# Eight experts' results: plain scatters into eight zeroed areas and additions on DVE, in place of accumulating scatters into one

## The reference

```python
k = max(MIN_CAPACITY, ceil(N * CAPACITY_FACTOR / E))   # N = 4096 tokens, E = 8: k = 1024
scores = softmax(xt @ Wr)
G, idx = top_k(scores.T, k)            # each expert takes its 1024 best tokens
X_in = xt[idx]
h = gelu(einsum('ekd,edh->ekh', X_in, W1) + b1)
X_e = einsum('ekh,ehd->ekd', h, W2) + b2
contrib = G[..., None] * X_e
out = zeros((N, D)).at[idx.reshape(-1)].add(contrib)
x = layernorm(x + out)
```

## Time and profile before

| | before |
|---|---|
| median of three runs | 719.66 us |
| span of the profiled execution | 715.9 us |
| PE busy | 577.3 us (81%) |
| DVE busy | 392.2 us (55%) |
| ACT busy | 324.2 us (45%) |
| POOL busy | 311.9 us (44%) |
| moved by DMA | 27.52 MB |

### The profile page before, as it was taken

One profiled execution on the slowest core, in us unless ns is written; L12 is line 12 of the kernel. 1 busy time (PEld: TensorE's weight loads), 2 busy tenths in 40 slices (PEclk: granted clock), 3 DMA queues, 4 the chain that ended last, 5 costly groups with the idle time before them and its releaser, 6 DMA issues.

```text
span 715.9 us, 11711 instructions
## 1 busy us (share of the span) xinstructions
PE 577.3 (81%) x3943; PEld 485.4 (68%) x3944; DVE 392.2 (55%) x942; ACT 324.2 (45%) x740; POOL 311.9 (44%) x309
## 2 busy tenths in 40 slices
PE   8899999999999999999998874017997688684700
PEld 7878889988998899889987761013775455552500
DVE  3237766675777677757766647886542240010206
ACT  3566755765676557656764321004431232131105
POOL 7103233322332333223323230017888788788756
PEclk9999999999999999999999995556997897897855
DMA  7000100001001000010000009001233233323347
GB/s 158 17 9 0 32 24 10 23 22 31 1 21 31 22 8 23 22 31 0 22 16 15 16 1 257 0 5 48 45 40 43 44 41 40 49 42 38 32 69 193
DMA packets 50066, 27.52 MB, mean 38 GB/s; under 512 B 14258, under 2 KB 46963, under 8 KB 50036
## 3 DMA queue, kind: packets, MB, share of 16 engines
q1 hardware_dynamic: 38144, 18.44, 9.8%
q0 software_dynamic: 11264, 8.66, 9.1%
q10 hardware_dynamic: 628, 0.03, 0.1%
HBM read 16.49 MB, written 10.62 MB: 38 GB/s over the span
## 4 chain that ended last, share of the span: by engine, by line
PE 42%; DVE 21%; POOL 15%; issue 13%; ACT 5%; DMA 3%; POOLq 0%; DVEq 0%; ACTq 0%
PE PS L1174 9%; POOL total L603 6%; POOL shared L593 6%; PE PS L1200 6%; PE PS L1414 6%; PE PS L1182 6%; PE PS L1396 3%; DVE csum L850 3%; PE PS L1191 3%; DVE pc L844 2%; DVE above L973 2%; DMA shared<-table,idx 2%; PE PS L1110 2%; DVE cmax L839 2%; ACT pc L672 1%
## 5 line engine op out<-in xcount | busy, mean ns | idle before, releaser
L568 POOL TENSOR_TENSOR pn<-pc,crcp 128x1232 f32<-128x1232 f32 x32 | 72.0, 2250 | 181.8 <-DVE crcp L853 181.8
L603 POOL DMA_INDIRECT total<-pn,idx x64 | 103.6, 1619 | 21.8 <-issue 18.0
L593 POOL DMA_INDIRECT shared<-table,idx x64 | 66.9, 1046 | 70.6 <-DVE idx L1031 51.4
L1174 PE MATMUL PS<-cT_hi,heads_hi 128*128 128x308 f32 x256 | 83.7, 327 | 1.2 <-DVE VOT L900 0.6
L652 ACT ACTIVATE shared<-PS 128x308 f32<-128x308 f32 (+1 forms) x144 | 62.0, 473 | 41.7 <-PE PS L1209 29.5
L1174 PE MATMUL PS<-cT_hi,heads_lo 128*128 128x308 f32 x256 | 77.9, 304 | 0.0
L1174 PE MATMUL PS<-cT_lo,heads_hi 128*128 128x308 f32 x256 | 77.4, 302 | 0.0
L1182 PE MATMUL PS<-shared,x1T 128*128 128x512 f32 (+1 forms) x192 | 72.4, 513 | 1.9 <-DVE pc L844 1.4
L1414 PEld LDWEIGHTS PS<-w,shared 128*128 128x128 f32 x512 | 71.0, 224 | 4.1 <-issue 3.8
L1414 PE MATMUL PS<-w,shared 128*128 128x128 f32 x512 | 72.2, 308 | 0.1
L787 ACT ACTIVATE shared<-PS,b1T 128x512 f32<-128x512 f32 x64 | 44.0, 687 | 60.3 <-PE PS L1396 60.3
(11 more groups left out here) (181 smaller groups left out, 1192.0 us busy)
## 6 DMA issues: line engine op xcount, KB each, us to landing
xin<-in_x SPq DMA_DIRECT2D x16, 128.0 KB, 2.1
table<-x SPq DMA_DIRECT2D x16, 128.0 KB, 2.0
total<-x SPq DMA_DIRECT2D x16, 128.0 KB, 1.9
w<-in_L_ffn_W SPq DMA_DIRECT2D x1, 2048.0 KB, 8.6
fin<-total SPq DMA_DIRECT2D x8, 256.0 KB, 5.0
out_x<-fin SPq DMA_DIRECT2D x8, 256.0 KB, 2.3
cin<-in_ctx SPq DMA_DIRECT2D x16, 77.0 KB
shared<-table,idx POOLq DMA_INDIRECT x64, 2.5
```

Source lines behind the costliest of these rows:

```text
L568: pool.tensor_tensor(pn[:, e, 0:HK].rearrange("p (h k) -> p h k", h=HEADS), pc[:, e, :].rearrange("p (h k) -> p h k", h=HEADS), crcp[:, e, ...
L593: pool.indirect_dma_start(xg[:, e % 3, h, :], None, table, bass.IndirectOffsetOnAxis(ap=idx[:, e, h:h + 1], axis=0)).then_inc(gathered[e % ...
L603: pool.indirect_dma_start(total, bass.IndirectOffsetOnAxis(ap=idx[:, e, h:h + 1], axis=0), ye[:, e % 2, h, :], None, compute_op=ALU.add).t ...
L1174: i = pe.matmul(bank[:, 0:4 * KEYS], w[a][:, h, :], cT[b][:, :], start=(n == 0), stop=(n == 2))
```

## The change

Each expert gets a DRAM area of its own, `spread[e]` (4096 rows of 128), in place of the one `total`. Eight parts:

1. POOL writes a tile `zeros` (128 x 512) among its constants, and ACT, behind its set-up copies and before its attention steps, issues eight DMAs that fill the eight areas with zeros from it, 2 MB each, in pieces of 2 KB (`cleared`).
2. SP no longer stores x2 to `total`, so `stored` counts 16 per pair, not 32.
3. Behind the gates' store SP loads x2 from `table` into `fin` in one DMA (`fin_x`).
4. The scatters are plain writes into `spread[e]`. Scatter(e) does not wait for scatter(e - 1) any more; scatter(0) waits for `cleared`. Two semaphores, by the parity of e, count the landings.
5. When the 8 blocks of expert e have landed, SP loads `spread[e]` in eight parts into `landed`, a view of `VOT` behind `yb`; from the second expert on each part waits until the same part of the expert before has been added.
6. DVE adds each part to `fin` (`add_landed`, 128 x 512): those of expert e - 2 stand in the program in halves behind `results(e, 0)` and `results(e, 1)`; those of expert 5 stand all before `last_results`, those of expert 6 behind it.
7. Those of expert 7 are put into the last loop, one part ahead of the statistics.
8. The eight loads of `total` at the end go.

```diff
+            act.wait_ge(consts, 19)
+            for e in range(E):
+                act.dma_start(spread[e].rearrange("(p a r) d -> p a (r d)", p=P, r=4),
+                              zeros[:, :].unsqueeze(1).to_broadcast([P, B // 4, 4 * P])).then_inc(cleared, 16)
             attention_steps(act, step)
...
                 sp.dma_start(tab[q, :, :, 0:P], x2[parity][:, :, :]).then_inc(stored[parity], 16)
-                sp.dma_start(sm[q], x2[parity][:, :, :]).then_inc(stored[parity], 16)
...
-            sp.wait_ge(scattered, 16 * SB * E)
-            rows = total.rearrange("(b t) d -> t b d", t=P)
-            for c in range(B // 4):
-                sp.dma_start(fin[:, 4 * c:4 * c + 4, :], rows[:, 4 * c:4 * c + 4, :]).then_inc(fin_in[c], 16)
+            sp.dma_start(fin[:, :, :], by_token[:, :, 0:P]).then_inc(fin_x, 16)
+
+            for e in range(E):
+                sp.wait_ge(scattered[e % 2], 16 * SB * (e // 2 + 1))
+                rows = spread[e].rearrange("(b t) d -> t b d", t=P)
+                for c in range(B // 4):
+                    if e:
+                        sp.wait_ge(landed_added, B // 4 * (e - 1) + c + 1)
+                    sp.dma_start(landed[:, 4 * c:4 * c + 4, :], rows[:, 4 * c:4 * c + 4, :]).then_inc(landed_in[c], 16)
...
-                if e:
-                    pool.wait_ge(scattered, 16 * SB * e)
+                if e == 0:
+                    pool.wait_ge(cleared, 16 * E)
                 for h in range(SB):
                     pool.wait_ge(ye_done, blocks_through(e, h))
-                    pool.indirect_dma_start(total, bass.IndirectOffsetOnAxis(ap=idx[:, e, h:h + 1], axis=0),
-                                            ye[:, e % 2, h, :], None, compute_op=ALU.add).then_inc(scattered, 16)
+                    pool.indirect_dma_start(spread[e], bass.IndirectOffsetOnAxis(ap=idx[:, e, h:h + 1], axis=0),
+                                            ye[:, e % 2, h, :], None).then_inc(scattered[e % 2], 16)
...
+            def add_landed(e, first, last):
+
+                if e == 0 and first == 0:
+                    dve.wait_ge(fin_x, 16)
+                for c in range(first, last):
+                    dve.wait_ge(landed_in[c], 16 * (e + 1))
+                    if e:
+                        dve.wait_ge(landed_added, B // 4 * (e - 1) + c + 1)
+                    dve.tensor_tensor(fin[:, 4 * c:4 * c + 4, :], fin[:, 4 * c:4 * c + 4, :],
+                                      landed[:, 4 * c:4 * c + 4, :], ALU.add).then_inc(landed_added, 1)
...
                 results(e, 0)
                 if e + 3 < E:
                     make_idx(e + 3)
+                if e >= 2:
+                    add_landed(e - 2, 0, B // 8)
                 results(e, 1)
+                if e >= 2:
+                    add_landed(e - 2, B // 8, B // 4)
+            add_landed(E - 3, 0, B // 4)
             last_results()
+            add_landed(E - 2, 0, B // 4)
...
+            add_landed(E - 1, 0, 1)
             for c in range(B // 4):
-                dve.wait_ge(fin_in[c], 16)
+                if c + 1 < B // 4:
+                    add_landed(E - 1, c + 1, c + 2)
+                dve.wait_ge(landed_added, B // 4 * (E - 1) + c + 1)
```

More of the change, by code:

```diff
@@ L297, in decoder_layer @@
         idx = sb("idx", [P, E, SB], I32)
-        yb = VOT[:, 0, 0:SB * P].rearrange("p (s d) -> p s d", s=SB)
+        votflat = VOT[:, :, :].rearrange("p b n -> p (b n)")
+        yb = votflat[:, 0:SB * P].rearrange("p (s d) -> p s d", s=SB)
+        landed = votflat[:, SB * P:SB * P + TOKENS].rearrange("p (b d) -> p b d", b=B)
+        zeros = sb("zeros", [P, 4 * P])
         stf = sb("stf", [P, B, 6])
@@ L373, in decoder_layer @@
         ye_done = sem("ye_done")
-        scattered = sem("scattered")
-        fin_in = [sem(f"fin_in{c}") for c in range(B // 4)]
+        cleared = sem("cleared")
+        scattered = [sem(f"scattered{k}") for k in range(2)]
+        fin_x = sem("fin_x")
+        landed_in = [sem(f"landed_in{c}") for c in range(B // 4)]
+        landed_added = sem("landed_added")
         fin_var = sem("fin_var")
@@ L383, in decoder_layer @@
         table = nc.dram_tensor("table", [TOKENS, ROW], F32, kind="Internal").ap()
-        total = nc.dram_tensor("total", [TOKENS, P], F32, kind="Internal").ap()
+        spread = [nc.dram_tensor(f"spread{e}", [TOKENS, P], F32, kind="Internal").ap() for e in range(E)]
         x_pairs = x.rearrange("(q e) t d -> q t e d", e=2)
@@ L487, in _ @@
             for k in range(2):
-                sp.wait_ge(stored[k], 32 * PAIRS // 2)
+                sp.wait_ge(stored[k], 16 * PAIRS // 2)
             sp.wait_ge(gates_done, 1)
-            sp.dma_start(table.rearrange("(b t) d -> t b d", t=P)[:, :, P:ROW], gates[:, :, :]).then_inc(gates_stored, 16)
-            sp.wait_ge(scattered, 16 * SB * E)
-            rows = total.rearrange("(b t) d -> t b d", t=P)
-            for c in range(B // 4):
-                sp.dma_start(fin[:, 4 * c:4 * c + 4, :], rows[:, 4 * c:4 * c + 4, :]).then_inc(fin_in[c], 16)
+            by_token = table.rearrange("(b t) d -> t b d", t=P)
+            sp.dma_start(by_token[:, :, P:ROW], gates[:, :, :]).then_inc(gates_stored, 16)
+            sp.dma_start(fin[:, :, :], by_token[:, :, 0:P]).then_inc(fin_x, 16)
[6 more added lines that the diff above has]
+                    sp.dma_start(landed[:, 4 * c:4 * c + 4, :], rows[:, 4 * c:4 * c + 4, :]).then_inc(landed_in[c], 16)
             for c in range(B // 4):
@@ L541, in _ @@
             pool.memset(keep[:, :, :], 1.0).then_inc(consts, 1)
+            pool.memset(zeros[:, :], 0.0).then_inc(consts, 1)
             pool.memset(onesb[:, :], 1.0).then_inc(consts, 1)
-            pool.wait_ge(consts, 18)
+            pool.wait_ge(consts, 19)
             pool.memset(keep[:, :, 0:1], 0.0).then_inc(consts, 1)
@@ L588, in gather @@
                     for k in range(2):
-                        pool.wait_ge(stored[k], 32 * PAIRS // 2)
+                        pool.wait_ge(stored[k], 16 * PAIRS // 2)
                 if e >= 3:
@@ L831, in second_norm @@
                     wait(dve, rstd2, 2 * q + e + 1)
-                    wait(dve, stored[par], 32 * earlier)
+                    wait(dve, stored[par], 16 * earlier)
                     dve.tensor_scalar(x2[par][:, e, :], r2[:, e, :], mv2[:, e, 0:1], rs2[:, e:e + 1],
@@ L1036, in last_results @@
                 e = E - 1
-                dve.wait_ge(scattered, 16 * SB * (e - 1))
+                dve.wait_ge(scattered[e % 2], 16 * SB * (e // 2))
                 for n in range(SB):
```

7 lines of the change are left out of this document (2 added, 5 removed).

## The result

The changed kernel takes 724.78 us, the median of four runs (723.59 to 726.51), beside 719.42 for the kernel before (718.54 to 719.85): a ratio of 1.0079, 95% interval 1.0055 to 1.0103. Slower, by 5.4 us where I had forecast 14.3. The profiled execution spans 722.5 us against 715.9. (Lines are renumbered: the gather is L604, the scatter L614, the additions L1083, the zeroing L775.)

The account below looks back on a forecast made before the run. Attention was taken as bound by PE, the expert stage by POOL's gathers and scatters, the tail by DVE. 715.9 - 23.5 + 38 = 730.4 us of span, plus 3.8, gave 734; range 697 to 746.

Parts of the forecast that it names:

- rival A: Before attention: ACT's queue fills and its zeroing issues hold it; 734 us, between 722 and 746; chance 0.62.
- the wait in front of the last scatter: Last expert: POOL waits 5 us, instead of 2.65, for expert 5's loads and additions before its final scatter.
- Scatter 0.945 us: Expert stage: a plain scatter takes POOL as long as a gather, 0.945 us instead of 1.552.
- Rival C: Expert stage: a plain scatter costs 1.55 us like the accumulating one, slower still, 769 or 733 us; chance 0.03.
- Stage 168.4 us: POOL, first gather to end of scatter 6: 168 us instead of 194.4, net -26 with 8 us of contention.
- Rival D: Expert stage: loads and additions bind, period stays 25 us, the 26 us gain is gone; 725 or 760; chance 0.03.
- The zeroing, +38: ACT before attention: eight 2 MB fills hold it until about 59 instead of 23.1, +36, plus 2 for PE.
- The rule: DMA issue on ACT: an issue ends when the backlog ahead has shrunk to 389 to 1611 packets.
- The restart of PE, +2: Start of attention: PE restarts from an idle spell with slower first matmuls, +2 us.
- Rival B: Before attention: the queue takes all eight fills at 0.5 us each, faster; 699 us, from 690 to 710; chance 0.28.
- The last expert, +2.5 (from -26 to -23.5): Final scatter and tail: longer wait and additions in the tail reduce the gain to -23.5 us, end at 692.4.
- Around the span: Whole kernel: the median of the runs lies 3.8 us above the profiled span.

Follow-up runs that it names:

- plain_in_before: Kernel before with the accumulation taken out of its scatters, areas, waits and stores unchanged; 715.8 us, ratio 0.9933 to the kernel before.
- small_adds: Changed kernel with each of DVE's 64 additions cut from 128x512 to 128x4; 752.5 us, ratio 1.0433 to the kernel before.
- after_again: Changed kernel run again unaltered on another chip; 758.0 us, ratio 1.048 to the kernel before.
- first comparison: First measurement of the changed kernel beside the kernel before, chip not on record; 724.8 us, ratio 1.0079.
- groups 1 to 5: Follow-up kernels, each group run on one chip beside the kernel before (2 and 3 shared a chip); the unaltered changed kernel took 751.8 to 758.0 us there.
- after_fourth: Changed kernel unaltered, one run as a control beside kernels with half the second layer's matmuls left out; 751.8 us.

## Why the prediction was wrong, step by step

The direction and the mechanism were right: rival A, the hold of ACT by its own queue, sets the result, and 724.78 lies within the 722 to 746 that I gave it. 734.0 itself was 9.2 us too high: I forecast a loss of 14.3 us, and it was 5.4. Two steps failed: the zeroing was sized at 38 us and cost 32.8, and the wait in front of the last scatter was put at 5 us and was 0.69. By the terms:

- **Scatter 0.945 us.** Measured 0.972; plain_in_before shows that it is the kind. Right. Rival C (1.55) is out.
- **Stage 168.4 us.** Measured 169.25. Right, with its 8 us of additions' contention: undisturbed 64 x 1.247 + 56 x 1.272 = 151.0, so 18.2 us are lost where 11.0 were, 7.2 us more; small_adds against after_again gives 6.6 for all additions. The Trainium skill ("SBUF — State Buffer", "Who interferes with whom") infers that the writing of descriptors isn't touched by such DVE work; 6.6 us of issue time of gathers and scatters speak against that.
- **Rival D** (loads and additions bind) is out: the DMA engines are at 0.47 in the stage, where I had 16 to 18 of 22 us, and waits for results ahead of scatters come to 2.8 us.
- **The zeroing, +38, measured +32.8.** This is the largest error. The rule was right: some 1362 pieces were left when the eighth issue ended, within 389 to 1611. (My three counts, too, include some of the small packets.) The size was not. I had 36 us of hold; it was 32.4. Of this, some 2 us are the amount, 11.9 MB and not the 12.7 of the middle, and some 1.6 the rate, 366 GB/s over the stretch and not 350: the 297 in my middle came from a stretch with 512-byte pieces on one side, which the fills don't have. Another 2.1 us are a slip: I added the hold to 23.1, where ACT was wanted, although ACT was free at 21.6 and its first issue began at 21.00. In the lower bound I had taken this idle time off. The first row alone would have given 12.7 / 0.398 = 31.9, close to 32.4, but by luck, since both numbers are too high. The restart of PE, +2, was about right: 30.3 of the 32.8 us are ACT's delay, and the other 2.5 fit the first matmuls behind it, whose granted clock was 0.50, the lower of its two levels, where the kernel before had 1.00 (23.1 to 25.7 us). Columns as in the earlier trace rows:

```profile
53.40:56.00 2.60, 1.50 (x6) 1.53 (x7) 0.48 (x1) 0.78 (x2) 0.00 (x0) 0.50 1.04 377
```

- **Rival B** (the queue takes all eight at once) is out. What the Trainium skill says in "DMA: Bandwidth & Descriptors" ("Issuing engines are not separate DMA queues"), that initiating is usually small beside the transfer, doesn't hold for transfers of this size behind each other: the later issues took 5.4 us each, as long as 2 MB need on the engines.
- **The last expert, +2.5 (from -26 to -23.5), measured -1.1.** I expected a wait of 5 us for the additions of expert 5; it was 0.69. They ended at 682.4, 10.8 us behind the end of the last gather's issue (671.65), not 15. The term that failed here is the 5 us that I added to the loads for POOL's transfers beside them. A likely reason, not tested, is that plain scatters are few packets: the whole of POOL's queue moved 4096, with accumulation 11264. The tail with its additions kept about the pace that I gave it: 2.07 us per group, and 24.2 us from the first landed load (698.3) to the end, where I had 25.1.
- **Around the span** I carried over 3.8 us; the median lies 2.3 above the profiled span.

Together: 5.2 us too high in the zeroing (5.7 in ACT's delay, the restart 0.5 too low), 3.6 in the last expert, 1.5 around the span, and 0.8 too low in the stage, some 9.4 for the 9.2. In both of the large ones I had rows near to the case and took a middle or added to them.

What no rival of mine held was the delays. I had PE at 19 us per expert against POOL's 22 and called that enough. It is enough in the first comparison. In groups 1 to 5 PE isn't done in that time, the gathers of the changed kernel stretch over 180 to 187 us instead of 157, and the change costs not 5 us but 31 (after_fourth) to 37 (after_again). Taking time off POOL made PE's pace the bound, and with it the kernel became sensitive to something that the kernel before had and could not show.

## What to carry to other kernels

An engine that issues many large transfers behind each other can be held by them: here, from the third fill of 2 MB on, each issue lasted as long as one such transfer needs. Put such fills on the engine that has nothing else to do, here SP, and spread them over steps with idle DMA. When a change takes the bound off one engine, look at the next engine's margin in traces of more than one chip, for idle time that nothing explains. And when an edit seems to cure a fault that only some chips show, run the unedited kernel beside it on the same chip: without that the cure isn't shown.

## What the runs showed of the hardware

- With fills of 2 MB in packets of 2 KB, ACT's issues took 0.6, 0.7, 3.9 and then 5.4 us each; the last ended with some 1362 of these packets waiting.
- A plain indirect scatter of 128 rows took 0.972 us of POOL, an accumulating one 1.552; together with the gathers the queue moved 4096 packets instead of 11264.
- Additions on DVE with both inputs in SBUF slow POOL's issue of indirect DMAs: 6.6 us for the 64 additions of this kernel (141.6 against 135.0).
- The same program took 724.8 us in one comparison and 751.8 to 758.0 in three others, on three chips, by gaps of PE and late releases of DVE and ACT, with waits of up to 15 us. The first of them starts behind 32 matmuls of 16 columns in 0.95 us, later ones also 20 us and more behind the last of these. With the 32 in four parts it took 724.6, on a chip on which the unsplit kernel was not run.
